# Issuing the stores of the query parts from ScalarE, a chunk later, in a language model tower on one Trainium2 core

## The reference

```python
def _L1_attn_ref(x, Wq, Wp, bp):
    xh = x.reshape(B, N, NUM_HEADS, DIM_HEAD)
    q = jnp.einsum('bnhd,hed->bnhe', xh, Wq)
    scores = jnp.einsum('bnhe,bmhe->bhnm', q, q) / NORM
    attn = jax.nn.softmax(scores, axis=-1)
    res = jnp.einsum('bhnm,bmhe->bnhe', attn, q)
    return res.reshape(B, N, D) @ Wp.T + bp
```

## Time and profile before

| | us |
|---|---|
| median of 3 runs | 1326.52 |
| lowest and highest | 1326.2, 1327.88 |
| the profiled execution, its own time | 1327.17 |
| its span, first to last instruction | 1325.5 |
| PE busy | 1137.3 (86% of the span) |
| DVE busy | 687.0 (52%) |
| ACT busy | 597.9 (45%) |
| POOL busy | 313.0 (24%) |
| mean granted TensorE clock | 0.924 |

### The profile page before, as it was taken

The page is one execution under the profiler, slowest core; times in us unless marked ns, Lnnn a source line. Parts: engine busy times, 40 slices in busy tenths (PEclk is TensorE's granted clock), DMA queues, the critical chain, the costliest instruction groups (busy, mean ns, idle before and its releaser), DMA issues. The chain is left out here.

```text
span 1325.5 us, 15359 instructions
## 1 busy us (share of the span) xinstructions
PE 1137.3 (86%) x4442; PEld 626.8 (47%) x4442; DVE 687.0 (52%) x1924; ACT 597.9 (45%) x985; POOL 313.0 (24%) x317
## 2 busy tenths in 40 slices
PE   5649999999999999999999997646988878778872
PEld 4414444444444444444444454423545445456661
DVE  2245445745563565456546753457877855422220
ACT  3335644554565356445544542433665552024341
POOL 5120100110011001101300110116003574437774
PEclk9769999999999999999999998776998778889896
DMA  3200110220011211102520000086551116159996
GB/s 94 100 17 0 44 44 25 84 76 18 26 67 52 63 44 44 67 8 75 180 81 0 17 0 0 5 187 100 98 97 56 70 61 209 60 136 184 171 230 121
DMA packets 57042, 99.82 MB, mean 75 GB/s; under 512 B 10359, under 2 KB 37843, under 8 KB 56728
## 3 DMA queue, kind: packets, MB, share of 16 engines
q1 hardware_dynamic: 37832, 56.20, 16.0%
q0 software_dynamic: 19152, 42.92, 12.5%
HBM read 55.60 MB, written 53.00 MB: 82 GB/s over the span
## 5 line engine op out<-in xcount | busy, mean ns | idle before, releaser
L605 PE MATMUL b_ring<-left 128*128 128x512 f32 x480 | 210.9, 592 | 0.0
L605 PE MATMUL b_ring<-right,left 128*128 128x512 f32 x480 | 208.6, 592 | 0.0
L1010 POOL TENSOR_TENSOR b_rstd<-b_veps,b_mhalf 128x4 f32<-128x4 f32 x32 | 32.7, 1022 | 637.7 <-DVE b_veps L1056 637.7
L605 PE MATMUL b_ring<-XT,b_wqkv 128*128 128x512 f32 x384 | 175.2, 600 | 6.9 <-DMA b_wqkv<-in_wqkv 6.9
L605 PEld LDWEIGHTS b_ring<-left 128*128 128x128 f32 x480 | 90.3, 190 | 109.1 <-issue 109.1
L605 PEld LDWEIGHTS b_ring<-right,left 128*128 128x128 f32 x480 | 90.0, 190 | 108.3 <-issue 101.8
L822 ACT ACTIVATE left<-b_ring,b_cur 128x512 f32<-128x512 f32 x128 | 88.0, 687 | 74.8 <-PE b_ring L605 59.6
L605 PEld LDWEIGHTS b_ring<-XT,b_wqkv 128*128 128x128 f32 x384 | 71.5, 193 | 86.0 <-issue 78.7
L1157 DVE RECIPROCAL b_mixing<-b_mixing 128x1024 f32<-128x1024 f32 x16 | 104.8, 6553 | 0.5
L1917 DVE TENSOR_REDUCE a_nmax<-a_pA 128x2 f32<-128x512 f32 x128 | 84.8, 688 | 37.6 <-PE a_pA L1613 34.8
L817 ACT ACTIVATE b_ffo<-b_ring,b_cur 128x512 f32<-128x512 f32 x32 | 22.0, 687 | 169.6 <-PE b_ring L605 157.8
(11 more groups left out here) (325 smaller groups left out, 1863.7 us busy)
## 6 DMA issues: line engine op xcount, KB each, us to landing
xe<-b_nil POOLq DMA_DIRECT2D x16, 1284.0 KB, 5.3
x_rows<-xe SPq DMA_DIRECT2D x32, 321.0 KB, 4.0
left<-in_w SPq DMA_DIRECT2D x8, 1024.0 KB, 5.3
x_wt<-in_wexp SPq DMA_DIRECT2D x16, 384.0 KB, 4.6
b_wqkv<-in_wqkv SPq DMA_DIRECT2D x4, 768.0 KB, 4.5
right<-qparts SPq DMA_DIRECT2D x16, 192.0 KB, 4.9
left<-qparts SPq DMA_DIRECT2D x16, 192.0 KB, 5.0
left<-in_wexp SPq DMA_DIRECT2D x6, 384.0 KB, 4.6
```

Source lines behind the costliest of these rows:

```text
L605: last = pe.matmul(bank[:, :], lhsT(k), rhs(k), start=(k == 0), stop=(k == n_k - 1))
L1010: pool.tensor_tensor(rstd[:, :], veps[:, :], mhalf[:, :], ALU.pow).then_inc(s_rs, 1)
```

## The change

The function `stored` goes from SP to ACT. For each chunk from 1 on, ACT issues the stores of the chunk before it, after it has written its own first part; those of the last chunk stand at the end. SP keeps its waits and the loads.

```diff
         @block.sync
-            def stored(c):
-                sp.wait_ge(s_p3, c + 1)
-                for s in range(CH // SEQ):
-                    sp.dma_start(g["qparts"][c * CH // SEQ + s].rearrange("i k p t -> p (i k) t"),
-                                 part[c][:, :, :, s * SEQ:(s + 1) * SEQ].rearrange("p i k t -> p (i k) t")).then_inc(s_st[c], 16)
-
-            stored(0)
             sp.wait_ge(s_full, PRODUCTS)
             sp.wait_ge(s_s2, ITEMS)
             sp.wait_ge(s_n, 2 * ITEMS)
             sp.wait_ge(s_st[0], 16 * CH // SEQ)
             operands_loaded(sp, g, 0)
-            stored(1)
             operands_loaded(sp, g, 1)
-            for c in range(2, NC):
-                stored(c)
             sp.wait_ge(s_st[1], 16 * CH // SEQ)
...
         @block.scalar
+            def stored(c):
+                act.wait_ge(s_p3, c + 1)
+                for s in range(CH // SEQ):
+                    act.dma_start(g["qparts"][c * CH // SEQ + s].rearrange("i k p t -> p (i k) t"),
+                                  part[c][:, :, :, s * SEQ:(s + 1) * SEQ].rearrange("p i k t -> p (i k) t")).then_inc(s_st[c], 16)
+
             rows_normalised(1, 0)
             query_columns_copied(0)
             rows_normalised(1, 1)
             for c in range(NC):
...
                 last.then_inc(s_p1, 1)
+                if c:
+                    stored(c - 1)
                 if c + 1 < NC:
                     query_columns_copied(c + 1)
                 act.wait_ge(s_qr1, c + 1)
                 act.activation(part[c][:, 1, :, :], rest, ACT.Copy).then_inc(s_p2, 1)
                 if c + 2 < NC:
                     rows_normalised(1, c + 2)
+            stored(NC - 1)
```

## The result

The changed kernel takes 1319.20 us in the median of 8 runs (1314.64 to 1321.29); before takes 1326.46 beside it (8 runs, 1322.72 to 1329.24). The ratio is 0.9945, with an interval from 0.9928 to 0.9962: faster by 5.0 to 9.6 us. I had forecast 1328.3 in a range from 1320.4 to 1330.5.

The account below looks back on a forecast made before the run. SP's issuing before the block's close was taken as the bound there; with packets in turn, +1.8 made 1327.17 us into 1329.0, and the median, 0.65 lower, 1328.3, range 1320.4 to 1330.5.

Parts of the forecast that it names:

- SP alone is last, and its end sets the close: End of first attention layer's block: all engines wait over ten microseconds for SP, which only issues, until 887.1 us.
- A shift of the close passes to the end one for one: Everything behind the block's close moves with it, with 1 us each way for the return of PE's clock.
- Chunk 0's stores 1.65 us later: ACT issues them after its chunk 1 copies, at 861.93 instead of 860.30, so SP's loads start at 866.2.
- 24 loads in 14.9 us: SP's operand loads before the close take 14.9 us to issue, as for the next two sequences, ending at 881.1.
- case 2: Stores get through at their own speed beside the loads: close 5.8 us earlier, 1320.7 us; chance 0.33.
- ACT's issues, 0.4 to 0.55: Each of the eight stores moved to ACT costs about what SP's nearest issues took, 0.4 to 0.55 us.
- The step that failed: Choosing the packets-in-turn end for two queues on 16 DMA engines: stores starve beside loads, PE starts 1.8 us later.
- The hold that the forecast feared: Chunk 2's second store, fourth in ACT's queue, held from 873 to 885.4 us, delaying the last chunk behind it.
- Below about four to one ... little is left: The gain of 5.8 us needs several store packets served per load packet; below this ACT returns at 885 or later.
- case 1: Engines take one packet of each queue in turn: PE starts 1.8 us later, 1328.3 us; chance 0.38.
- My estimate by the Trainium skill's round-robin: Engines alternate between queues, some 13 store runs against a load's 3: block's close about 1.5 us later than now.
- Case 4, one order for both queues: Engines serve in order of issue, SP's loads held behind ACT's stores; change does nothing, 1326.0 us; chance 0.14.

Follow-up runs that it names:

- the last experiment: Against the kernel before: chunk 0 stored by SP, chunk 1 by ACT; sequence 1's loads and chunks 2 and 3's stores by SP in the next block; 1316.79 us.

## Why the prediction was wrong, point by point

- *SP alone is last, and its end sets the close*: right, shown from both sides. Taking issues off SP by any way (ACT, or SP later) gains what they took until the next engine is last; in the last experiment that was DVE, at the place the profile of before gave.
- *A shift of the close passes to the end one for one*: right; 6.5 against 6.5 in the means of two.
- *Chunk 0's stores 1.65 us later*: wrong, nothing within the 0.3 of the reference. I had put ACT's issue behind the end of the copies before it. The trace shows it going out before they begin, 0.04 us after DVE's part. So it was also wrong that only the last wait for DVE is real: the issues for chunks 0, 1 and 2 all went out right behind it.
- *24 loads in 14.9 us*: 16.5, and 16.3 in the second profile. I had taken away the slow issues behind stores because the stores left the queue. They stay slow when the stores come by ACT's.
- These two errors, 1.65 too much and 1.6 too little, cancel. That case 2's close came out right (5.8 forecast, 5.5 and 6.1 measured against the first profile of before) is in this part luck.
- *ACT's issues, 0.4 to 0.55*: 0.39 to 0.79. Right.
- **The step that failed** is the one that began "I take the second end, because the engines' share is full while loads run and packets differ eightfold in size: a share by packets starves the small ones." From a full share I had concluded how it is divided. In the changed kernel chunk 1's stores stood for 2.8 us, then got 15 packets to one of the loads, and landed 6.7 us after issue; the forecast needed 18. Chunk 2's second store was not held (0.56, forecast some 12), and everything behind it fell away: chunk 1's stores had landed at 874.9, just behind its issue. The hold that the forecast feared exists, as the doubled stores show, but the change has none. Its terms were off: I had the fourth store come back with 75 packets an engine out; with doubled stores it came back with 50 and 47 out (806 and 759 packets on 16 engines), after 2.96 and 5.99 us.
- In case 2, "Below about four to one ... little is left" was wrong too: from 867.8 to 883 ACT's queue moved 3121 packets to 804 of SP's, 3.9 to one, and the whole gain was there. When the stores get through counts, not only their share.
- A slip in case 1's sum: 51 packets at 24 ns from 884.7 end at 885.9, not 886.4. Case 1's time hangs on ACT's chain and is not touched by it.
- My estimate by the Trainium skill's round-robin, page "DMA: Bandwidth & Descriptors", section "Queues, rings and completion order", had 13 store rows to 3 load rows. The trace has 5 packets to 159, 15 to 1 and 0.6 to 1 in three stretches of one execution, so no fixed number a turn describes it, and the close 1.5 us later did not come.
- *Case 4, one order for both queues*: partly seen. SP's issues slow down behind ACT's stores, and the landing of a store follows what was issued ahead of it (3.8 against 6.7). But SP is delayed by 1.6 us, not by the 5 that case 4 needed.

Open stays what decides whose packets the engines take. An order close to that of issue fits chunk 1's stores (3.8 and 6.7) and the stretches in which stores stood nearly still, from 880 in the change and with doubled stores, where the loads issued before them were being served. It does not fit chunk 2's second store in the change. No run separates the making of the descriptors from the taking of turns.

## What to carry to other kernels

At a point where all engines meet, look at who comes last, and if it is an engine that only issues, count what it must issue before that point and what could as well stand after it. Moving it later on the same queue gave as much here as moving it to another engine, and moving more of it gave more. And where a forecast hangs on how two queues share busy engines, a full busy share says nothing about the division: give both ends, and say that nothing read so far chooses between them. Here the share swung between nearly nothing and 15 to one within a few microseconds.

## What the hardware showed that I had not expected

- ACT issues a DMA ahead of activations that stand before it in its program: the issue went out at 861.98, 0.04 us after what its semaphore waited for, while the copies before it ran from 862.55.
- The hold of an issue goes by the rows waiting, not by bytes, as far as one kernel shows: with 48 rows of 512 B an engine for each store, the fourth in a row took 2.96 and 5.99 us on ACT and 3.42 on SP; spare copies of twice the bytes of a store in 8 rows an engine took 1.45 at most.
- Behind a pair of stores on ACT's queue SP's issues are slow: 1.04 and 1.43 us behind chunk 1's, 0.91 and 0.87 behind chunk 2's, where 0.59 is usual. Twice the stores did not slow them more.
- Two profiles of one kernel differ by 0.6 to 3.1 us in the place of this close (32.1 and 31.5; 37.6 and 39.0; 34.9 and 31.8). In the two wider pairs the profile with the later close has the longer hold or the more slow issues (four stores in 6.76 us instead of 5.42; six slow issues instead of two).
